# Feed of each state into PSUM, four normalisings on ScalarE, residues formed by TensorE, weights in two groups, and a new slot table, in a one-core hybrid of a state-space block, a gated recurrence and two expert layers

## Chip, core and metric

The program runs on one core of a Trainium2 chip. Time is device microseconds of one execution. All arrays are fp32, except a bf16 split of one small tile and the bf16 masks of the expert layers. TensorE is written PE, VectorE DVE, ScalarE ACT, GpSimd POOL and SyncE SP.

## What is computed

The input x is 16 batches of 512 tokens of 128 features. Each batch passes four stages; only the core of each is shown.

```python
# A: state-space block
xn = x * rsqrt(mean(x*x) + 1e-5) * norm_w      # of x already layer-normalised
u, res = split(xn @ in_proj_w.T, 2)
u_c = silu(causal_conv4(u))                    # 256 channels
dt_r, Bm, Cm = split(u_c @ x_proj_w.T)         # 8, 16, 16
delta = softplus(dt_r @ dt_w.T + dt_b)
for n in 16 states:                            # scan along the 512 tokens
    h[n] = exp(delta * A[n]) * h[n] + (delta * u_c) * Bm[n]
y = sum_n(h[n] * Cm[n]) + u_c * Dp
out = (y * silu(res)) @ out_proj_w.T + x
z = gelu(out @ ff_w1.T) @ ff_w2.T + out;  a = layernorm(z) * w + b
# E (twice, called e1 and e2): one expert of 8192 for each of 8 heads, by product keys
q = layernorm(x) @ w_q;  pick = argmax over 32 keys, for 16 groups
x += sum_h( relu(score_h) * gelu(<w_down[pick_h], layernorm(x)>) * w_up[pick_h] )
# B: gated linear recurrence with 16 states, tanh, projection, layernorm (between e1 and e2)
```

## The kernel before

Every engine runs its own program over the same list of iterations (`run_pipeline`). Iteration i does phase PRE of batch i+1, phase CORE of batch i and phase POST of batch i-1 and of the three before it. An iteration has 64 slots (`TURN`), four for each state n of the scan. The table `SLOTS` gives each stage of each engine its slot, written out in the file; a slot of 64 or more means that the stage runs one or more iterations later. Thus five batches are in flight. `LAST_SLOTS` holds other slots for the last iterations, 16 to 19, in which only POST is left. An engine executes its own stages in slot order, one after the other, and waits on semaphores of the others. Slots of two engines are not tied together otherwise.

In PRE the batch is loaded and its statistics are taken. DVE normalises it (`dve_norm_x`, L1094), PE transposes it (L658) and forms the convolution as four matmuls for each half (L754), ACT applies silu, and PE projects to `dbl`. ACT writes `dbl` in bf16 into `split`, and POOL (`pool_rest`, L1335 and L1337) forms the two residues that make the bf16 split exact to three parts. POOL also forms `delta` (L1340) and `du` = delta * u_c (L1344).

In CORE, state n takes five steps. ACT forms dA = exp(delta * A[n]) (L925), four states ahead. PE spreads row n of B over all partitions into one of three PSUM banks `bcast` (`spread`, L716), and row n of C likewise; the three banks serve B and C in turn. In slot 4n DVE scans hp in place with dA (L1187), in slot 4n+1 it feeds the next state, hp = du * B (`feed`, L1177), and in slot 4n+2 it multiplies by C (L1196). For states 1, 9 and 11 POOL does that multiplication (L1318), from a copy of the row that ACT makes. PE adds the product to `ysum` through an identity matmul (L733). Four hp buffers rotate.

In POST the layernorms before e1, e2 and B are also applied by DVE (L1094). DVE finds the maxima (L1111, L1118) and the indices (L1126 to L1143). POOL issues 8 indirect DMAs for each of four token tiles and each expert layer, 64 in an iteration (L1305). DVE forms the dot products with the fetched rows (L1150), ACT scales the other half of each row (L907), and PE sums them (L692). Banks 0, 1 and 2 of PSUM are taken in turn by these stages; `claim` makes PE wait until the last user of a bank has been read.

All 37 weight loads come first. Setup waits for all of them, folds some weights (L534 to L564, PE L583 to L592), and only then does iteration -1 begin.

The few lines of the scan and the feed:

```python
nc.vector.tensor_tensor_scan(flat, dA[...], flat, 0.0, ALU.mult, ALU.add).then_inc(scanned, 1)
...
dve.wait_ge(b_spread, at(c, NS, n))
dve.wait_ge(y_sum, at(c, NS, before[-1]))
nc.vector.tensor_tensor(hp[:, BUFFER[n], :, :], src[:], spread_tile(0, n), ALU.mult).then_inc(fed, 1)
```

## Time and profile before

| what | value |
|---|---|
| median of three runs | 2453.9 us (2447.63 to 2456.02) |
| the profiled execution | 2438.47 us |
| its span, first to last instruction | 2436.5 us |
| mean granted TensorE clock | 0.859 of full speed |
| DVE busy | 2043.8 us, 84% |
| PE busy | 1641.8 us, 67% |
| POOL busy | 1572.4 us, 65% |
| ACT busy | 1322.6 us, 54% |

The profiled execution is 15 us shorter than the median of the three; 2 us of it lie outside the span. The shares are means over a start of some 70 us, a long middle, and an end of 354 us in which only POST is left. Busy time of an engine is a union: instructions of one engine overlap a little, so count times mean duration is more than it.

### The profile page before, as it was taken

What the parts mean: (1) busy time and instruction counts of PE and PEld (TensorE: products, weight loads), DVE (VectorE), ACT (ScalarE), POOL (GpSimd) and SP (SyncE); (2) the same over time, 40 slices, a digit from 0 to 9 for tenths busy, and PEclk for the clock granted to TensorE, in tenths of its full rate; (3) what the DMA queues carried; (4) which work ended last, traced back from release to release, by engine and by line L of the source; (5) the groups of instructions that cost most, each with busy time, mean ns of one, the idle gap of its engine ahead of it and who ended that gap; (6) DMA issues with size and microseconds to landing.
All of it is one profiled execution on the core that took longest, in us unless ns stands there. A gap on an engine that the chain in (4) does not pass through costs nothing.

```text
span 2436.5 us, 22230 instructions
## 1 busy us (share of the span) xinstructions
PE 1641.8 (67%) x5130; PEld 895.1 (37%) x5130; DVE 2043.8 (84%) x4871; ACT 1322.6 (54%) x2634; POOL 1572.4 (65%) x1175
## 2 busy tenths in 40 slices
PE   4677667677677867687787677787777767434532
PEld 2232334343334434343344344343444433322321
DVE  2899888899999999999999899999999898433332
ACT  2543555547475657575574757574766655212522
POOL 0135454686868686887868686868778786735344
PEclk9799898889898989998898889898999888766766
DMA  2001111121222222222212122222222121312122
GB/s 48 9 5 35 48 35 43 35 80 52 83 59 78 59 81 69 67 78 59 81 51 81 55 82 58 78 67 76 76 58 76 51 84 58 102 52 74 44 67 76
DMA packets 79859, 150.38 MB, mean 62 GB/s; under 512 B 20585, under 2 KB 46593, under 8 KB 79681
## 3 DMA queue, kind: packets, MB, share of 16 engines
q0 software_dynamic: 49152, 134.28, 19.1%
q1 hardware_dynamic: 28048, 13.90, 2.1%
q10 hardware_dynamic: 2544, 1.09, 0.3%
q14 instruction: 94, 0.76, 0.1%
q8 instruction: 21, 0.34, 0.1%
HBM read 145.01 MB, written 4.19 MB: 61 GB/s over the span
## 4 chain that ended last, share of the span: by engine, by line
DVE 33%; POOL 27%; issue 18%; PE 11%; ACT 4%; another core or an unknown queue 3%; DMA 1%; DVEq 0%; POOLq 0%; ACTq 0%
POOL rows L1305 24%; DVE hp L1187 8%; DVE rows L1150 5%; DVE hp L1177 3%; PE ysum L733 3%; DVE hp L1196 3%; PE bank L692 2%; DVE top L1111 2%; POOL hp L1318 2%; DVE mask L1132 2%; ACT rows L907 2%; DVE mask L1126 1%; PE bank L754 1%; DVE rank L1134 1%
## 5 line engine op out<-in xcount | busy, mean ns | idle before, releaser
L1305 POOL DMA_INDIRECT rows<-in_experts,index x1024 | 1276.4, 1246 | 428.0 <-issue 305.7
L733 PE MATMUL ysum<-hp,ident 128*128 128x512 f32 x1024 | 552.7, 667 | 120.3 <-POOL hp L1318 61.5
L1187 DVE TENSOR_TENSOR_SCAN hp<-dA,hp 128x1024 f32<-128x1024 f32 x256 | 591.2, 2309 | 7.4 <-issue 6.5
L925 ACT ACTIVATE dA<-delta,decay 128x511 f32<-128x511 f32 x512 | 334.9, 711 | 146.0 <-DVE hp L1187 101.2
L716 PE MATMUL bcast<-split,pick 128*128 128x512 bf16 x512 | 182.4, 409 | 288.4 <-DVE hp L1177 263.9
L1177 DVE TENSOR_TENSOR hp<-du,bcast 128x1024 f32<-128x1024 f32 x256 | 308.2, 1204 | 69.1 <-POOL du L1344 47.8
L1150 DVE CUSTOM_DVE_ANT_0 rows<-rows,xn 128x128 f32<-128x128 f32 x1024 | 303.8, 361 | 57.5 <-DMA rows<-in_experts,index 53.5
L733 PEld LDWEIGHTS ysum<-hp,ident 128*128 128x128 f32 x1024 | 211.1, 210 | 313.2 <-issue 145.4
L907 ACT ACTIVATE rows<-rows,coef 128x128 f32<-128x128 f32 x1024 | 307.6, 388 | 1.8 <-DVE coef L1157 1.8
L863 ACT ACT_TABLE_LOAD x215 | 275.8, 1283 | 15.4 <-PEq L500 11.7
L692 PE MATMUL bank<-rows,ident 128*128 128x256 f32 x1024 | 245.3, 395 | 42.0 <-ACT rows L907 42.0
L1196 DVE TENSOR_TENSOR hp<-hp,bcast 128x1024 f32<-128x1024 f32 x208 | 252.2, 1213 | 0.1
L1335 POOL TENSOR_TENSOR soft<-dbl,split 128x512 f32<-128x512 f32 x16 | 31.5, 1968 | 326.5 <-ACT split L1011 326.5
L692 PEld LDWEIGHTS bank<-rows,ident 128*128 128x128 f32 x1024 | 205.5, 201 | 73.9 <-ACT rows L907 42.5
L716 PEld LDWEIGHTS bcast<-split,pick 128*128 128x128 bf16 x512 | 52.0, 102 | 434.8 <-DVE hp L1177 318.8
L675 PE MATMUL bank<-w_sim,xnT 128*128 128x512 f32 x256 | 160.2, 712 | 17.7 <-DVE mask L1118 11.5
L1318 POOL TENSOR_TENSOR hp<-hp,c_row 128x1024 f32<-128x1024 f32 x48 | 121.6, 2533 | 32.7 <-ACT c_row L942 26.4
L868 ACT ACTIVATE ln<-mv,eps 128x4 f32<-128x4 f32 x48 | 14.3, 297 | 229.4 <-DVE mv L1080 147.5
L1111 DVE TENSOR_REDUCE top<-bank 128x16 f32<-128x512 f32 x128 | 86.5, 676 | 46.3 <-PE bank L675 42.8
L754 PE MATMUL bank<-xrT,w_taps 128*128 128x512 f32 x256 | 116.8, 599 | 1.6 <-ACT ucs L999 0.8
L1118 DVE TENSOR_TENSOR mask<-bank,top 128x512 bf16<-128x512 f32 x128 | 88.6, 692 | 13.1
L900 ACT ACTIVATE x<-bank 128x256 f32<-128x256 f32 x64 | 24.2, 379 | 133.5 <-PE bank L692 97.5
(171 smaller groups left out, 2267.6 us busy)
## 6 DMA issues: line engine op xcount, KB each, us to landing
rows<-in_experts,index POOLq DMA_INDIRECT x1024
x_in<-in_x SPq DMA_DIRECT2D x16, 256.0 KB
x_res<-in_x SPq DMA_DIRECT2D x16, 256.0 KB
y<-x SPq DMA_DIRECT2D x16, 256.0 KB
rows<-in_wq_t ACTq DMA_DIRECT2D x1, 512.0 KB
rows<-in_taps SPq DMA_DIRECT2D x1, 512.0 KB
rows<-in_in_proj_t SPq DMA_DIRECT2D x1, 256.0 KB
rows<-in_key_t SPq DMA_DIRECT2D x1, 128.0 KB
```

Source lines behind the costliest of these rows:

```text
L692: mm = nc.tensor.matmul(total, ident[:], e.rows[:, tiles, h, P:2 * P], start=False, stop=(h == HEADS - 1), skip_group_check=True)
L716: nc.tensor.matmul(bcast[k % NBC][:, 0, :], pick[:, r:r + 1].to_broadcast([P, P]), part[:], start=True, stop=True).then_inc((b_spread, c_s ...
L733: mm = nc.tensor.matmul(ysum[:, j, :], ident[:], hp[:, BUFFER[k], j, :], start=(k == 0), stop=(k == NS - 1))
L863: act.preload_act_table_set(name)
L907: op = nc.scalar.activation(row, row, ACT.Copy, scale=e.coef[:, t, h:h + 1])
L925: op = nc.scalar.activation(dA[:, n % NDA, j, 1:T], delta[q][:, j, 1:T], ACT.Exp, scale=decay[:, j, n:n + 1])
L1150: op = nc.vector.tensor_tensor_reduce(row, row, e.xn[:, t, :], 1.0, 0.0, ALU.mult, ALU.add, e.dot[:, t, h:h + 1])
L1177: nc.vector.tensor_tensor(hp[:, BUFFER[n], :, :], src[:], spread_tile(0, n), ALU.mult).then_inc(fed, 1)
L1187: nc.vector.tensor_tensor_scan(flat, dA[:, n % NDA, :, :].rearrange("p a b -> p (a b)"), flat, 0.0, ALU.mult, ALU.add).then_inc(scanned, 1)
L1196: nc.vector.tensor_tensor(state, state, spread_tile(1, n), ALU.mult).then_inc(read_out, 1)
L1305: pool.indirect_dma_start(e.rows[:, t, h, :], None, A["experts"], bass.IndirectOffsetOnAxis(ap=e.index[:, t, h:h + 1], axis=0)).then_inc(e ...
L1318: pool.tensor_tensor(state, state, c_row[:, k % NCR, :].unsqueeze(1).to_broadcast([P, NH, T]), ALU.mult).then_inc(pool_read, 1)
```

## The change

It has six parts.

1. **Feed.** `feed` writes du * B into a new PSUM tile of two banks, `fed_ps`, and the scan reads it there and writes hp. So the wait for `y_sum` moves from the feed to the scan, and the feed of state n+1 waits for the scan of state n. B has one PSUM bank (`b_ps`) and C one (`c_ps`), in place of three for both. Only two banks are left for all other stages: those of bank 2 move to bank 1, and the sum of e2 moves to bank 0.
2. **Normalising.** The four tiles xr, xn of e1, xn of e2 and xnb are written by ACT (`Identity` with scale and bias). DVE only forms the bias, -mean * scale.
3. **Residues.** PE subtracts the bf16 parts in the PSUM bank of `dbl` with a matmul by minus the identity (`pe_rest`), and ACT reads them there. POOL's two subtractions go. The dt matmuls now follow the two residues in bank 0.
4. **Loads.** Eleven loads that PRE needs come first. The other 26 are issued by SP as iteration -1 begins. Folding is done by PE and DVE at the end of iteration -1, and the taps are scaled in its slot 6.
5. **Smaller setup.** Only the first column of dA is cleared.
6. **Slot tables.** All of `SLOTS` and `LAST_SLOTS` is new.

```diff
+        b_ps = ctx.enter_context(nc.psum_tensor("b_ps", [P, 1, T], F32))
+        c_ps = ctx.enter_context(nc.psum_tensor("c_ps", [P, 1, T], F32))
+        fed_ps = ctx.enter_context(nc.psum_tensor("fed_ps", [P, NH, T], F32))
-        bank = [ctx.enter_context(nc.psum_tensor(f"bank{k}", [P, T], F32)) for k in range(3)]
+        bank = [ctx.enter_context(nc.psum_tensor(f"bank{k}", [P, T], F32)) for k in range(2)]
...
     # DVE, feed
+                    if n:
+                        dve.wait_ge(scanned, at(c, NS, n - 1))
-                    nc.vector.tensor_tensor(hp[:, BUFFER[n], :, :], src[:], spread_tile(0, n),
+                    nc.vector.tensor_tensor(fed_ps[:], src[:], b_ps[:].to_broadcast([P, NH, T]),
                                             ALU.mult).then_inc(fed, 1)
     # DVE, scan
+                        if before:
+                            dve.wait_ge(y_sum, at(c, NS, before[-1]))
-                        nc.vector.tensor_tensor_scan(flat, dA[:, n % NDA, :, :].rearrange("p a b -> p (a b)"), flat,
-                                                     0.0, ALU.mult, ALU.add).then_inc(scanned, 1)
+                        nc.vector.tensor_tensor_scan(flat, dA[:, n % NDA, :, :].rearrange("p a b -> p (a b)"),
+                                                     fed_ps[:].rearrange("p a b -> p (a b)"), 0.0, ALU.mult,
+                                                     ALU.add).then_inc(scanned, 1)
...
     # PE, slot 4n
-                        for k in range(2 * n + 3, min(2 * n + 5, 2 * NS)):
-                            spread(c, split[q], k)
+                        spread_c(c, split[q], n)
+                        if n + 1 < NS:
+                            spread_b(c, split[q], n + 1)
...
+                    for m, r, k in due("pe_rest", i, q, slot):
+                        claim(0, i)
+                        nc.tensor.matmul(bank[0][:], minus[:], split[r][:], start=False, stop=True,
+                                         skip_group_check=True).then_inc(rest_mm, 1)
+                        fill(0, i, m, "pe_rest", k, (part2, split_done)[k], 1)
...
     # ACT
+                    for m, r, _ in due("act_norm_x", i, q, slot):
+                        act.wait_ge(p_shifted, at(m, 1))
+                        if later(m):
+                            act.wait_ge(p_turned, at(m - 1, 1))
+                        normalise(xr, x_in, s20, offx, p_normed)
...
     # slots that the text speaks of
-    "pe_sum_e2": (POST, (243, 250)),
+    "pe_sum_e2": (POST, (248, 248)),
-    "dve_dot_e1": (POST, (61, 71, 76, 80)),
+    "dve_dot_e1": (POST, (56, 74, 76, 77)),
-    "dve_index_e2": (POST, (194, 203)),
+    "dve_index_e2": (POST, (177, 191)),
-    "pool_rest": (PRE, (35,)),
-    "pool_delta": (PRE, (48,)),
+    "pool_delta": (PRE, (50,)),
-    "pool_x1": (POST, (0,)),
-    "pool_x3": (POST, (113,)),
-    "pool_fetch_e1": (POST, (37, 47, 51, 52)),
+    "pool_x1": (POST, (11,)),
+    "pool_x3": (POST, (124,)),
+    "pool_fetch_e1": (POST, (42, 44, 52, 53)),
```

## Rows read from the trace of the kernel before

**Rows 1.** The page, part 2: DVE's busy tenths in 40 slices of the span.
```profile
DVE  2899888899999999999999899999999898433332
```

**Rows 2.** Stretches: us, then busy us (instructions) of PE, PEld, DVE, ACT, POOL.
```profile
0.00:73.50 73.50, 31.02 (x78) 16.51 (x78) 16.57 (x57) 24.33 (x37) 8.26 (x11) 0.85 0.20 40
...
758.80:1824.90 1066.10, 800.18 (x2546) 439.98 (x2545) 1025.60 (x2417) 665.59 (x1320) 807.46 (x585) 0.90 0.24 69
...
2082.60:2436.50 353.90, 132.62 (x440) 89.14 (x438) 118.45 (x613) 102.94 (x271) 169.11 (x176) 0.67 0.24 68
```

**Rows 3.** DVE's groups, 758.8 to 1824.9 us: busy us, mean ns, idle before.
```profile
L1187 DVE TENSOR_TENSOR_SCAN hp<-dA,hp 128x1024 f32<-128x1024 f32 x128 | 292.3, 2283 | 6.5 <-issue 6.5
L1150 DVE CUSTOM_DVE_ANT_0 rows<-rows,xn 128x128 f32<-128x128 f32 x512 | 162.2, 382 | 14.0 <-DMA rows<-in_experts,index 14.0
L1177 DVE TENSOR_TENSOR hp<-du,bcast 128x1024 f32<-128x1024 f32 x128 | 154.3, 1206 | 3.3 <-PE bcast L716 3.0
...
L1132 DVE TENSOR_TENSOR mask<-mask 128x512 bf16<-128x512 bf16 x32 | 25.5, 797 | 1.1
...
L1094 DVE TENSOR_SCALAR xr<-x_in,mv,s 128x128 f32<-128x128 f32 x32 | 20.4, 714 | 0.3
L1094 DVE TENSOR_SCALAR xn<-x,mv,rs 128x128 f32<-128x128 f32 x64 | 18.6, 372 | 0.0
...
L1094 DVE TENSOR_SCALAR xnb<-x,mvB,rsB 128x128 f32<-128x128 f32 x32 | 8.8, 370 | 0.0
```

**Rows 4.** DVE's groups over the whole span: the small bias instruction.
```profile
L1088 DVE SCALAR_TENSOR_TENSOR off<-mv,rs 128x4 f32<-128x4 f32 x16 | 2.5, 157 | 0.0
```

**Rows 5.** Single lines over the whole span: ns min/median/max, first and last start.
```profile
L1150 DVE CUSTOM_DVE_ANT_0 rows<-rows,xn x1024: 258/286/4226, 241.4 to 2417.1; 128x128 f32<-128x128 f32 x171
...
L1132 DVE TENSOR_TENSOR mask<-mask x64: 424/426/2641, 210.2 to 2382.6; 128x512 bf16<-128x512 bf16 x64
...
L1305 POOL DMA_INDIRECT rows<-in_experts,index x1024: 943/949/3087, 214.9 to 2411.9; - x171
```

**Rows 6.** Timeline of DVE and POOL: start us, duration us, engine, line.
```profile
781.12 2.28 DVE L1187 TENSOR_TENSOR_SCAN hp<-dA,hp 128x1024 f32<-128x1024 f32 x1
783.32 0.66 DVE L1111 TENSOR_REDUCE top<-bank 128x16 f32<-128x512 f32 x1
784.09 0.69 DVE L1118 TENSOR_TENSOR mask<-bank,top 128x512 bf16<-128x512 f32 x1
...
781.71 2.44 POOL L1305 DMA_INDIRECT rows<-in_experts,index  x1 [0.31 <-issue]
...
882.97 2.42 POOL L1344 TENSOR_TENSOR du<-delta,ucs 128x1024 f32<-128x1024 f32 x1 [0.16 <-POOL delta L1340]
...
883.12 2.42 DVE L1150 CUSTOM_DVE_ANT_0 rows<-rows,xn 128x128 f32<-128x128 f32 x1
```

**Rows 7.** POOL's groups, 758.8 to 1824.9 us.
```profile
L1305 POOL DMA_INDIRECT rows<-in_experts,index x513 | 665.4, 1297 | 167.7 <-issue 148.2 <-DVE index L1143 18.9
...
L1335 POOL TENSOR_TENSOR soft<-dbl,split 128x512 f32<-128x512 f32 x8 | 14.0, 1750 | 83.5 <-ACT split L1011 83.5
```

**Rows 8.** ACT's and PE's groups, 758.8 to 1824.9 us.
```profile
L875 ACT ACTIVATE xn<-x_in,off,rs 128x128 f32<-128x128 f32 x32 | 13.1, 478 | 0.0
...
L733 PE MATMUL ysum<-hp,ident 128*128 128x512 f32 x513 | 275.9, 665 | 46.8 <-DVE hp L1196 29.6 <-POOL hp L1318 17.0
...
L716 PE MATMUL bcast<-split,pick 128*128 128x512 bf16 x256 | 89.5, 401 | 141.4 <-DVE hp L1177 132.8 <-issue 8.3
```

**Rows 9.** Timeline of the start: start us, duration us, engine, line.
```profile
15.97 0.49 DVE L534 TENSOR_SCALAR rows<-rows,norm_w 128x512 f32<-128x512 f32 x1 [7.14 <-DMA w_xproj<-in_xproj_t]
...
28.18 0.87 DVE L1075 BATCH_NORM_STATS2 st<-x_in 128x6 f32<-128x128 f32 x4 [0.32 <-PEq L500]
...
34.30 5.16 PE L754 MATMUL bank<-xrT,w_taps 128*128 128x512 f32 x8 [0.78 <-ACT xrT L993]
...
73.54 2.29 DVE L1187 TENSOR_TENSOR_SCAN hp<-dA,hp 128x1024 f32<-128x1024 f32 x1 [0.53 <-ACT dA L925]
```

625 lines of the change are left out of this document (324 added, 301 removed).

## The prediction, made before the changed kernel was seen to run

> **What bounds the kernel now.** I read the page's slices first: DVE is busy nine tenths or more in nearly every slice from the seventh to the 33rd, and drops to three or four tenths at the end [rows 1]. So there are three stretches, and I asked for the busy time of each [rows 2]. In the middle I took 758.8 to 1824.9 us. It holds 128 scans, 16 to an iteration, so eight iterations of 1066.1 / 8 = 133.3 us [rows 2, 3]. DVE is busy 1025.6 / 8 = 128.2 us of each and idle 5.1. PE is busy 100 us, POOL 101, ACT 83. DVE sets the pace of the middle. At the start (73.5 us) all engines together follow one chain from the weights to the first scan. At the end (354 us) no engine is busy half the time: that is a chain of latencies, and DVE's work is only 118 us of it [rows 2].
>
> Second, POOL is fuller than it looks. Between two indirect DMAs of the same group lie 0.3 us of issue that count as idle: 64 x (1.297 + 0.30) = 102 us, with 101 - 64 x 1.297 = 18 us of other work 120, and a wait of 83.5 / 8 = 10.4 us at the first residue [rows 7]. Together that is the iteration.
>
> Third, DVE and POOL stop each other. An indirect DMA takes 949 ns in the median but 1297 on average, and up to 3087 [rows 5, 7]; the one that starts 0.6 us into a scan takes 2.44 us and ends after it [rows 6]. In the other direction, a dot product takes 286 ns in the median, 382 on average; the one that starts beside POOL's `du` takes 2.42 us [rows 5, 6]. In both cases the DVE instruction has two inputs in SBUF. Feed and C product, one input in PSUM, take 1206 ns without such cases [rows 3].
>
> **The change, part by part.** Per iteration of the middle, on DVE:
>
> Normalising. The three groups are busy 20.4 + 18.6 + 8.8 = 47.8 us in eight iterations, 6.0 each [rows 3]. Each of the four sets overlaps the next instruction by some 0.1 us, as the scan does (next start 2.20 after its own, duration 2.28 [rows 6]), so 5.5 us go. This contains the stops of xr (714 ns against 372 of xn). Four small instructions come, 4 x 0.157 = 0.6 us [rows 4], less overlap: +0.5. ACT gets 16 instructions of 478 ns at most [rows 8], 7.6 us beside its 50 idle ones, so they cost nothing there. On the chain to the transposes they are 0.4 to 0.8 us slower a set; those chains have a state of slack or more in the middle. With that cover gone, at the end, three sets for each of four batches cost up to 10 us.
>
> Stops of DVE by POOL. The dots lose 512 x (382 - 286) = 49.2 us in the eight iterations, the mask maximum 32 x (797 - 426) = 11.9 [rows 3, 5]: 7.6 us an iteration. They happen where POOL's tensor products meet dots or masks. Two of POOL's eight products go (residues). The new table puts the first dots at slot 56 behind `pool_delta` at 50, where they were at 61 behind 48, and the others at 10, 12, 13 away from the products of slots 0 and 4, which now fall into scans. But `pool_x1` at 11 is beside the dots, and `dve_index_e2` at 49 and 63 is beside `pool_delta` and `pool_x3`. I can't see the new meeting points, so: bounds 0 and 7.6, and I take 5, since the scan no longer shifts POOL's work to random places.
>
> Scan and feed. If one input in SBUF does not stop POOL, as feed and C product show, the 348 ns of mean excess go from each DMA: 64 x 0.348 = 22 us of POOL, and with the residues (about 3 us and the wait of 10) POOL falls from 133 to about 97 us. That shortens nothing by itself; it makes fetches early. The Trainium skill, page "SBUF — State Buffer", section "Who interferes with whom", states that a DVE instruction with two SBUF inputs contends with a GpSimd instruction that reads SBUF and one with a single SBUF input outside the two-port modes does not; the trace agrees, with the 2.44 us above.
>
> The price of a PSUM output or of a scan out of PSUM is in no row. The nearest are feed and C product, 1206 to 1213 ns with PSUM in, for 1024 elements, where the scan of two SBUF inputs has 2283; nothing in them asks for more than 15 ns. I take +15 ns on 32 instructions, 0.5 us; bounds 0 and 0.1 us each, 3.2 us. The feed must wait for the scan before it. Where it stands right behind it, it loses the overlap of 0.08 and gains a gap of 0.11, as the mask behind the maximum does (783.32 + 0.66 to 784.09 [rows 6]): 0.19. By the new table twelve of sixteen slots 4n have another DVE stage between them: 4 x 0.19 = 0.8 us. The upper bound is 16 x 0.19 = 3.0.
>
> PE. Spreads were a whole state ahead; DVE waited for them only 3.0 us in eight iterations [rows 3], while PE waited 132.8 us for feeds [rows 8]. Now B of n+1 can be spread only in slot 4n, behind the C product of n-1, and is wanted right after scan n. PE has 2.28 us for two spreads of 0.4, so 1.4 to spare, and the other stages of slot 4n; what it still has to do of earlier slots must fit in. A state has 8.3 us, PE's mean work is 6.3, of which `ysum` is some 2. States 4 (skip and a convolution half) and 14 (both halves of e2's sum, 18 matmuls, then y) are heavier than their DVE time by 2 to 3 us. I put +3 us on DVE's idle time of 5.1; bounds 0 and 12. The residue matmuls add two of the spread's kind, under 1 us, to PE.
>
> Sum per iteration: -5.5 + 0.5 - 5 + 0.5 + 0.8 + 3 = **-5.7 us**, so 127.6 us. Eleven iterations of that kind: -63. The filling ones before have fewer POST stages; five at half of it or a little more: -14. The last one with a scan: -5. Middle: -82.
>
> Start. Statistics begin at 28.18, held by the loads (15.97) and the folding [rows 9]. After, setup ends when six DMAs per queue and 4 us of memsets are done: about 6. From there to the first convolution matmul it took 34.30 - 28.18 = 6.1. Now the taps stand in between: 11 loads, the last issued at about 4 instead of 11 us, land some 5 us later, at 9; tap scaling 2 us; shift, ACT set, transpose and copy 4 more: convolution at about 15.3, which is -19. The residues move in front of dt: two rounds of a spread-like matmul and an ACT copy of 0.6, +2.3. Folding took 28.2 - 16.0 = 12 us; it now lies behind PE's dt matmuls and beside ACT's exp and log and POOL's two products, which hide all but some 2 us (all 12 if that cover is gone). Start: -15. The 26 later loads are issued by SP while nothing waits for it.
>
> End. Other slots, sums of three stages in one bank, a slower ACT set, but nothing whose size I can read: 0, bounds -15 and +15.
>
> Total: -82 - 15 = **-97 us**. Against the profiled execution that is 2438.5 - 97 = 2341; against the median, 15 us higher, **2357 us**.
>
> **Rivals.** *More of the same* (0.15): all stops go (-2.6 more) and idle stays at 5.1 (-3): 5.6 x 17 = 95 us more at most, half of it likelier: 2262 to 2310. *The stops only move* (0.12): POOL's products meet other dots; the 5 us stay, +85: 2437. The table speaks for it, since `pool_x1`, `pool_x3` and `pool_delta` still have two-input neighbours. Here also stands the case that the scan goes on stopping POOL. *PSUM has a price* (0.08): the 0.1 us of the bound, 2.7 us more an iteration, +45: 2402. The Trainium skill, page "VectorE: DVE Perf Modes", section on the TRN2 errata, gives 62 more fixed cycles to an instruction from PSUM than to one from SBUF; by that estimate 65 ns on 32 instructions give 2.1 us an iteration. Our rows of PSUM inputs do not bear it out, and no row has a PSUM output.
>
> *PE is late* (0.10), the case on the other side. With one bank for B and one for C, every wait of PE for ACT (sigmoid, tanh, residues, bank 1 held by five stages in turn) that comes before slot 4n delays feed and C product. Without idle growth the gain is 97 + 3 x 17 = 148 us, or 148 / 256 = 0.58 us for each state. If DVE waits longer than that on average, 9 us an iteration, the kernel is slower. Four late states of 3 us would do: 12 us, then 2454 - 148 + 12 x 17 = 2510. PE's 33 idle us speak against it, the lost lead of a state for it.
>
> **Numbers.** The forecast's own case, 2315 to 2400, has 0.52; the rivals 0.45; 0.03 is left for no change. The measurement of this kernel can't tell less than about 0.3%, 7 us, from nothing. Only the late PE ends above; the moved stops end at -0.7%. Faster 0.87, same 0.03, slower 0.10. The range of 8 in 10 goes from half of "more" to the moved stops: 2290 to 2435.
>
> **What would show it.** In the changed profile: iterations near 127 us; no L1305-like DMA above 1.3 us beside a scan, mean near 0.97; POOL's issue-corrected time near 97 us; mean dot near 310 ns; scan and feed within 30 ns of 2283 and 1206; DVE waiting for spreads some 3 us an iteration; first scan near 58 us; the end near 354. Wrong would make me: DVE idle above 14 us an iteration with PE as releaser, scans above 2.4 us, or dots as slow as before.

## The result: 12.9% slower here, and what the profile after shows

The changed kernel took 2764.51 us (median of four runs, 2761.82 to 2767.47) against 2450.77 for the kernel before beside it: 1.129 times as long, 95% interval 1.124 to 1.134. The forecast was 2357 us, with 0.87 on faster. It was wrong, and by far. The jobs of this study (a job is one set of kernels run side by side on one chip) fell under two conditions: under the first, called starving below, the kernel before took 2444 to 2454 us and the changed kernel 1.129 of it; under the second, called free, they took 2366 us and 0.941 of it, and all runs of a kernel in a job lay within 1%.

The first lines are of the page of the changed kernel, part 2 (busy tenths in 40 slices, cf. [rows 1]) and part 4 (who ends the chain).

```profile
DVE  3898999594986759578585957759597785834331
...
issue 4%; DVE 3%; PE 3%; ACT 2%; another core or an unknown queue 1%; POOL 1%; DMA 0%; ACTq 0%; POOLq 0%; DVEq 0%
```

VectorE was full from the seventh slice on; now it falls to five tenths every few slices. The chain adds up to 15% of the span only (97% in the kernel before), so nothing more is read from it. The next view has stretches of the same kernel, in the columns of [rows 2]: eight iterations, then one uninterrupted run of 32 indirect DMAs inside one of them, then the 6 us behind that run.

```profile
794.80:2099.00 1304.20, 826.79 (x2520) 446.37 (x2560) 968.07 (x2322) 693.16 (x1433) 607.57 (x568) 0.84 0.20 57
1140.20:1180.00 39.80, 12.38 (x55) 7.23 (x54) 16.54 (x68) 9.76 (x21) 30.35 (x32) 0.75 0.36 102
1180.00:1186.00 6.00, 0.00 (x0) 0.00 (x0) 0.51 (x3) 1.34 (x2) 0.04 (x1) 0.50 0.08 25
```

An iteration is 1304.2 / 8 = 163.0 us instead of 133.3. VectorE works 968.1 / 8 = 121.0 of it, 7.2 us less than before (forecast 8.7); but it is idle for 42.0. POOL works 76. In the 39.8 us in which POOL issues 32 DMAs, VectorE is busy 16.5, TensorE 12.4 and ScalarE 9.8: each is idle for more than half of it, and the granted clock falls with them to the lower level behind it (0.50).

The groups of VectorE and POOL in the eight iterations, in the columns of [rows 3] and [rows 7]:

```profile
L1235 DVE TENSOR_TENSOR_SCAN hp<-dA,fed_ps 128x1024 f32<-128x1024 f32 x128 | 291.5, 2278 | 5.0 <-issue 3.2 <-ACT dA L920 1.8
L1219 DVE TENSOR_TENSOR fed_ps<-du,b_ps 128x1024 f32<-128x1024 f32 x129 | 157.9, 1224 | 48.7 <-remote 37.5 <-PE b_ps L686 7.9
L1245 DVE TENSOR_TENSOR hp<-hp,c_ps 128x1024 f32<-128x1024 f32 x104 | 125.9, 1210 | 57.0 <-remote 44.3 <-issue 12.7
L1156 DVE CUSTOM_DVE_ANT_0 rows<-rows,xn 128x128 f32<-128x128 f32 x512 | 117.6, 287 | 61.4 <-issue 61.3
...
L1156 DVE DVE_READ_ACCUMULATOR2_ANT dot<- 128x1 f32 x512 | 42.1, 82 | 54.5 <-issue 54.5
```

```profile
L1350 POOL DMA_INDIRECT rows<-in_experts,index x512 | 493.4, 964 | 207.8 <-issue 148.0 <-DVE index L1149 57.9 <-DVE hp L1235 0.6
```

The durations are those of the forecast: scan 2278 (before 2283), dot 287 (382), indirect DMA 964 (1297). The idle time is what is new, and its releasers are not engines: "issue" and "remote" mean that the profile shows nothing of this core that the instruction waited for. They are weaker evidence than they look: in this trace most records of semaphore events are missing (see "What stays open"). TensorE as releaser has 7.9 us in eight iterations. The timeline of VectorE in that run of 32 (start us, duration us) shows what it looks like:

```profile
1153.36 0.29 DVE L1156 CUSTOM_DVE_ANT_0 rows<-rows,xn 128x128 f32<-128x128 f32 x1
1153.57 0.08 DVE L1156 DVE_READ_ACCUMULATOR2_ANT dot<- 128x1 f32 x1
1153.75 0.29 DVE L1156 CUSTOM_DVE_ANT_0 rows<-rows,xn 128x128 f32<-128x128 f32 x1
1155.20 0.08 DVE L1156 DVE_READ_ACCUMULATOR2_ANT dot<- 128x1 f32 x1 [1.16 <-issue]
...
1173.43 0.08 DVE L1156 DVE_READ_ACCUMULATOR2_ANT dot<- 128x1 f32 x1 [1.12 <-issue]
1174.82 0.29 DVE L1156 CUSTOM_DVE_ANT_0 rows<-rows,xn 128x128 f32<-128x128 f32 x1 [1.31 <-issue]
1176.24 0.08 DVE L1156 DVE_READ_ACCUMULATOR2_ANT dot<- 128x1 f32 x1 [1.12 <-issue]
1185.49 0.89 DVE L1088 BATCH_NORM_STATS2 stC<-bank 128x6 f32<-128x128 f32 x4 [9.17 <-remote]
```

Until 1153.6, 13.4 us into POOL's run, dots follow each other every 0.21 us. Then one instruction starts every 1.40 us (1173.43, 1174.82, 1176.24), although the rows have landed. The run ends at 1180.0; at 1185.5 the engine works normally again. The same happens at each run of 32, VectorE idle for 23.1 to 23.6 us in it and 5.4 to 5.6 after; a run of 16 costs 7.6 to 8.1 + 3.1, or 4.5 + 2.1 where one of its DMAs was stopped, one of 8 some 0.5. Together that is 38 us an iteration.

**Theory A:** a long uninterrupted run of indirect DMAs starves the other engines. In the kernel before, scans with two inputs in SBUF stopped POOL every 8 us and so cut its runs to 8 or fewer; the feed into PSUM took that brake away. ("Cut" means here that a DMA is stopped, not that POOL pauses: by the traces both kernels issue 32, 16, 8 and 8 DMAs in an iteration with 0.3 us between them. In the kernel before 6 or 7 of the 32 are stopped and take some 1.9 to 3.1 us, no more than 8 follow one another unstopped, and the row takes 49 to 51 us; in the changed kernel none is stopped and it takes 39.8.) **Theory B:** the single-bank spreads, TensorE's order or the merged banks cause the idle time, which falls beside the runs by chance.

### The profile page after: what moved, and what is told of

Read it like the earlier page. It is cut to its first block and busy times, and to the rows that moved or that the text cites. A ratio compares the mean times of both kernels' runs of the same rounds, so it can differ in the third digit from the quotient of the medians.

```text
span 2760.0 us, 22210 instructions
## 1 busy us (share of the span) xinstructions
PE 1688.4 (61%) x5088; PEld 907.6 (33%) x5162; DVE 1947.9 (71%) x4680; ACT 1382.0 (50%) x2859; POOL 1215.6 (44%) x1143
## 5 line engine op out<-in xcount | busy, mean ns | idle before, releaser
L1350 POOL DMA_INDIRECT rows<-in_experts,index x1024 | 986.1, 963 | 487.7 <-issue 300.2
L1235 DVE TENSOR_TENSOR_SCAN hp<-dA,fed_ps 128x1024 f32<-128x1024 f32 x256 | 583.1, 2278 | 5.5 <-issue 3.2
L1219 DVE TENSOR_TENSOR fed_ps<-du,b_ps 128x1024 f32<-128x1024 f32 x256 | 313.4, 1224 | 90.6 <-remote 52.8
L1156 DVE CUSTOM_DVE_ANT_0 rows<-rows,xn 128x128 f32<-128x128 f32 x1024 | 241.0, 294 | 132.9 <-issue 105.7
L1245 DVE TENSOR_TENSOR hp<-hp,c_ps 128x1024 f32<-128x1024 f32 x208 | 251.9, 1211 | 80.6 <-remote 57.2
L626 PE MATMUL bank<-w_y_ln,xnbT 128*128 128x128 f32 x128 | 42.8, 438 | 389.5 <-DVE stC L1088 378.1
L626 PEld LDWEIGHTS bank<-w_y_ln,xnbT 128*128 128x128 f32 x128 | 34.0, 326 | 400.5 <-DVE stC L1088 388.9
L686 PE MATMUL b_ps<-split,pick 128*128 128x512 bf16 x255 | 108.9, 427 | 71.2 <-DVE fed_ps L1219 48.9
L1156 DVE DVE_READ_ACCUMULATOR2_ANT dot<- 128x1 f32 x1024 | 84.2, 82 | 89.2 <-issue 89.2
L733 PE MATMUL bank<-xrT,w_taps 128*128 128x512 f32 x256 | 128.4, 648 | 23.1 <-issue 12.0
L695 PE MATMUL c_ps<-split,pick 128*128 128x512 bf16 x184 | 79.5, 432 | 81.7 <-DVE hp L1245 80.6
## 6 DMA issues: line engine op xcount, KB each, us to landing
rows<-in_key_t SPq DMA_DIRECT2D x1, 128.0 KB, 5.0
```

The costliest lines, as they stand in the source:

```text
L733: mm = nc.tensor.matmul(bank[0][:], w_taps[:, tap, k * P:(k + 1) * P], xrT[:, tap:tap + T], start=(tap == 0), stop=(tap == NK - 1))
L1156: op = nc.vector.tensor_tensor_reduce(row, row, e.xn[:, t, :], 1.0, 0.0, ALU.mult, ALU.add, e.dot[:, t, h:h + 1])
L1219: nc.vector.tensor_tensor(fed_ps[:], src[:], b_ps[:].to_broadcast([P, NH, T]), ALU.mult).then_inc(fed, 1)
L1235: nc.vector.tensor_tensor_scan(flat, dA[:, n % NDA, :, :].rearrange("p a b -> p (a b)"), fed_ps[:].rearrange("p a b -> p (a b)"), 0.0, ALU ...
L1245: nc.vector.tensor_tensor(state, state, c_ps[:].to_broadcast([P, NH, T]), ALU.mult).then_inc(read_out, 1)
L1350: pool.indirect_dma_start(e.rows[:, t, h, :], None, A["experts"], bass.IndirectOffsetOnAxis(ap=e.index[:, t, h:h + 1], axis=0)).then_inc(e ...
```

## Experiments

Each job compared its kernels with the kernel before on the same chip. The last column is the stretch of us behind the last gate, from the profile; a gate is the product with silu(res), once a batch (L1290 in the kernel before, L1335 in the changed one). Job 0 is the comparison above.

| job | kernel before | run | ratio (95% interval) | per iteration | end |
|---|---|---|---|---|---|
| 0 | 2450.8 | the changed kernel | 1.129 (1.124-1.134) | 163.0 | 340 |
| 1 | 2366.0 | e1_sbuf_feed | 0.968 (0.966-0.970) | 127.5 | 274 |
| 1 | | e2_paced | 1.262 (1.260-1.264) | 169 | 434 |
| 1 | | e3_before_paced | 1.348 (1.346-1.351) | 183 | 442 |
| 1 | | e4_tied | 1.012 (1.010-1.014) | 138.2 | 272 |
| 2 | 2444.0 | e5_pause4 | 0.989 (0.988-0.991) | 132.6 | 337 |
| 2 | | e6_pair_each | 1.773 (1.770-1.776) | 253 | 680 |
| 2 | | e7_pause1 | 0.951 (0.948-0.954) | 126.5 | 319 |
| 3 | 2452.1 | e8_pause1_core | 0.960 (0.957-0.964) | 126.5 | 333 |
| 3 | | e9_drain_core | 0.956 (0.953-0.959) | 128.0 | 337 |
| 3 | | e10_before_core | 1.086 (1.083-1.090) | 149.2 | 350 |
| 4 | 2365.7 | e11_after_again | 0.941 (0.939-0.942) | 124.9 | 270 |
| 4 | | e12_sbuf_again | 0.970 (0.968-0.973) | 128.2 | 276 |
| 4 | | e13_pause16 | 0.950 (0.948-0.951) | 124.5 | 293 |
| 4 | | e14_before_end | 1.021 (1.020-1.023) | 133.1 | 332 |
| 5 | 2365.5 | e15_pause16_again | 0.951 (0.949-0.952) | 124.7 | 294 |

m1_bench ran in job 2, m2_bench in job 3, m3_bench_again in job 5, each once. Jobs 0, 2 and 3 fell under the starving condition, jobs 1, 4 and 5 under the free one.

### Job 1: feed back in SBUF, pauses, fetches tied to scans

e1_sbuf_feed undoes one part of the change:

```diff
-nc.vector.tensor_tensor(fed_ps[:], src[:], b_ps[:].to_broadcast([P, NH, T]),
+dve.wait_ge(y_sum, ...)          # as in the kernel before
+nc.vector.tensor_tensor(hp[:, BUFFER[n], :, :], src[:], b_ps[:].to_broadcast([P, NH, T]),
                         ALU.mult).then_inc(fed, 1)
```

> The changed kernel with one part undone: the feed writes its product in place into the state's tile in SBUF, so that the scan reads both its inputs from SBUF again (and the feed waits for the state's output again); the PSUM spreads, the normalising on ScalarE, the residues and the slot table stay those of the changed kernel. Theory A: VectorE's idle time of 40 us in an iteration comes from GpSimd, which nothing stops any more, so that it issues 16 or 32 indirect DMAs in one uninterrupted run; from about 12 us into such a run all other engines nearly cease to be given instructions. Scans with two SBUF inputs stop GpSimd again for some 2.3 us each, every 7.7 us, so the runs are cut into pieces of at most 8 DMAs: iterations of 130 to 137 us instead of 159 to 167, time 2380 to 2460 us. Theory B: the idle time comes from the single-bank spreads, the order of TensorE's work or the merged banks: all of these are still there, so the iterations stay at 155 us or more and the time at 2680 to 2780 us.

e2_paced adds pauses to the changed kernel, e3_before_paced the same to the kernel before:

```diff
                 for h in range(HEADS):
                     pool.indirect_dma_start(...)
+                for _ in range(20):
+                    pool.memset(pause[:], 0.0)
+                    pool.drain()
```

> The changed kernel with one addition: after each 8 indirect DMAs GpSimd clears a small tile of its own 20 times, with a drain after each, a pause estimated at 3 to 8 us (8 pauses in an iteration, 24 to 64 us of GpSimd, which is idle over 80 us of each iteration). Nothing else is changed; the outputs are the same. Theory A (uninterrupted runs of indirect DMAs starve all engines from about 12 us on): no run lasts longer than 10 us before its pause, so VectorE's idle time of 40 us in an iteration goes to 8 to 15 us, iterations are 128 to 138 us, and the time 2330 to 2450 us, faster than the changed kernel by 300 us or more although only work was added. Theory B (spreads, TensorE's order, banks): a pause on GpSimd can only make rows later: 2760 us or more. If the pause is too short to let the other engines recover, something between, with the idle time per run smaller than 28 us for the run of 32.

> The kernel before with the same addition: after each 8 indirect DMAs GpSimd clears a small tile 20 times with a drain after each. Theory A: in its iterations the scans already cut the runs into pieces of 8, so the pauses give nothing there (GpSimd is busy 101 us of 132, and 8 pauses of 3 to 8 us can make its rows late: 0 to +100 us in all); but at its end, where no scan runs, a run of 32 DMAs left VectorE idle for 32 us, and with pauses this run costs 10 to 20 us less. So the end from the last gate on, 354 us, gets shorter by 10 to 25 us. Theory B: the end stays at 354 us or gets longer by the pauses.

e4_tied:

```diff
                     for m, r, t in due("pool_fetch_e2", i, q, slot):
+                        if CORE in has:
+                            pool.wait_ge(scanned, at(b[CORE], NS, n))
                         fetch(e2, m, t)
```

> The changed kernel with one addition: in the iterations each group of 8 indirect DMAs first waits for the scan of its slot's state, and the four groups of the second expert layer are set at slots 204, 212, 220 and 222 instead of 206, 211, 221 and 222, so that the groups come at least one state (7.5 us) apart where the table puts them apart; no pause lies between groups whose slots are of one state. Theory A: runs of 32 go away, leaving runs of at most 16 (7.6 us idle within and 3 after for one of 16): VectorE idle 12 to 25 us in an iteration instead of 40, time 2380 to 2560 us. Theory B: groups that start later can only make the dots later: 2760 us or more.

The SBUF feed gave 0.968, on the side of theory A but better than it had: iterations of 127.5 us (130 to 137 expected), 2289 us (2380 to 2460). The pauses came out slower than anything theory A allowed. POOL's timeline explains that: the first drain behind DMAs takes some 2.1 us, each further pair 0.30, so 20 pairs cost 8 us; eight of them an iteration, 64 us, on top of POOL's own 95 make 159 of 169 us. Both paced kernels were bound by POOL; the end of e3_before_paced, 442 us, tells nothing of starving for the same reason. At this point I read the job as for theory A, in particular because "issue" and "remote" as VectorE's releasers had vanished in e2_paced. That reading was too early, as job 4 shows: job 1 was under the free condition, where the changed kernel has only 3 us of such idle time an iteration without pauses either. For the same reason neither e1_sbuf_feed nor e4_tied tells the theories apart here. What e4_tied does show is a price: groups tied to scans make rows late (VectorE waits 96 us in eight iterations for fetched rows), 138.2 us an iteration.

### Job 2: shorter pauses, and a small kernel of dense streams

The same edit with 4 pairs after each 8 DMAs, with 1 pair after each 8, and with 1 pair after every DMA.

> The changed kernel with a pause of 4 clear-and-drain pairs after each 8 indirect DMAs (20 pairs took 8.5 us, so 4 take an estimated 1.7 us; 8 pauses in an iteration add 14 us to GpSimd's 76). Theory A: if 1.7 us is enough for the other engines to be supplied again, VectorE's waits named issue and remote (some 38 us in an iteration) vanish and rows are late by little: iterations of 125 to 135 us, ratio to the kernel before 0.95 to 1.00. Theory A': the supply needs the 5 us that passed after the end of each run before the engines went on: then 1.7 us brings back only a part, ratio 1.03 to 1.12. Theory B (20 pairs took the idle away by another way, such as GpSimd being late): a ratio of 1.10 or more.

> The changed kernel with a single clear-and-drain pair (0.43 us) after each 8 indirect DMAs. If any gap between DMAs resets the starving: starved time near zero, ratio 0.95 to 0.99, the best of the paced ones. If the gap must be as long as a stalled supply needs: starved time of 25 to 38 us an iteration, ratio 1.07 to 1.13.

> The changed kernel with one clear-and-drain pair (0.43 us) after every indirect DMA, so that a DMA starts each 1.7 us instead of each 1.25 and a run of 32 lasts 54 us instead of 40; 64 pairs add 27 us to GpSimd's 76 of an iteration. Theory A with the mean rate as the cause (each DMA uses up some of a budget that refills with time): the starved time falls but the rows are later: ratio 0.97 to 1.08. Theory A with the bare back-to-back issue as the cause (any other instruction on GpSimd between two DMAs lets the others in): starved time zero, ratio 0.95 to 1.00. If neither rate nor gaps matter: 1.12 or more.

A single pair after each 8 DMAs, which only adds work, has a ratio of 0.951 (2319 us) where the changed kernel without it had 1.129. The stretch of eight iterations in it, and what one pause is on POOL:

```profile
731.40:1743.00 1011.60, 781.02 (x2560) 409.25 (x2560) 940.48 (x2322) 694.32 (x1433) 619.62 (x632) 0.96 0.25 73
```

```profile
1324.21 0.95 POOL L1351 DMA_INDIRECT rows<-in_experts,index  x1 [0.30 <-issue]
1325.16 0.20 POOL L1355 MEMSET pause<- 128x100 f32 x1
1327.52 2.35 POOL L1369 TENSOR_TENSOR hp<-hp,c_row 128x1024 f32<-128x1024 f32 x1 [2.17 <-issue]
```

The iteration is 126.5 us, VectorE idle for (1011.6 - 940.5) / 8 = 8.9 of it. A gap of 2.6 us between groups of 8 DMAs takes away 33 us of idle time. Four pairs, 3.5 us, already make rows late (132.6 us); a pair after every DMA makes each DMA 3.5 us long, 64 x 3.5 = 224 us of POOL, and the iteration 253: 1.773, far above the 0.95 to 1.08 that I expected, so this run says nothing of starving.

The small kernel m1_bench has nothing of the reference in it; its output is only zeros. In stages it starts three streams of independent short instructions together with a run of 32 indirect DMAs:

```diff
+for j in range(ops):    # VectorE, 0.13 us each; ScalarE and TensorE alike
+    nc.vector.tensor_reduce(out_dve[:, j:j + 1], src[:, 0:width], AX_X, ALU.add)
```

> A small kernel of its own (the output is only zeros; nothing of the reference is computed): stages, each started together on all engines, in which GpSimd issues 32 indirect DMAs (128 rows of 1 KB each) while VectorE, ScalarE and TensorE work through streams of short instructions that wait for nothing. A row of an expert table is read as before. Stages: no DMA; 32 DMAs beside all three dense streams; 32 beside 40 wide reductions (1024 elements, some 1.1 us each) on VectorE alone; 32 beside 400 narrow ones on VectorE alone; 32 with rows of 128 B; 32 with 2 or 5 clear-and-drain pairs after each 8; 32 with one pair after each. Theory A1 (a long run holds up the supply of instructions, and each engine lives on what it has fetched): the narrow streams stop some 5 to 15 us into the run and go on after it (a stage of 30 us becomes 45 to 60 us), the 40 wide reductions take the same 44 us as without DMAs or at most 3 us more; pauses restore the supply. Theory A2 (the run stops any instruction, however long): wide reductions show gaps too, 10 us or more in all. Theory A3 (the bytes do it): rows of 128 B leave the streams undisturbed, against A1 and A2, by which the number of DMAs counts and the narrow rows disturb as much. Theory B (nothing of this is from the DMAs): all stages of dense streams take the same time within 2 us.

Windows of it: no DMA; 32 DMAs beside the three streams (the run alone, then the whole stage); 32 beside 40 wide reductions alone; beside 400 narrow ones alone; rows of 128 B; 2 pairs and 5 pairs after each 8 DMAs; one pair after each DMA.

```profile
3.20:50.90 47.70, 47.69 (x400) 47.53 (x400) 38.08 (x300) 22.00 (x150) 0.00 (x0) 1.00 0.01 2
51.00:91.10 40.10, 13.00 (x73) 11.18 (x74) 13.21 (x84) 14.97 (x80) 30.41 (x32) 0.62 0.35 102
51.00:135.00 84.00, 52.53 (x400) 50.39 (x400) 40.94 (x300) 25.73 (x150) 30.41 (x32) 0.76 0.17 51
148.80:194.00 45.20, 0.49 (x2) 0.30 (x2) 45.16 (x40) 0.26 (x1) 30.26 (x32) 0.54 0.32 93
194.00:272.60 78.60, 0.80 (x2) 0.50 (x2) 54.02 (x401) 0.27 (x2) 30.26 (x32) 0.50 0.19 54
289.20:372.30 83.10, 56.36 (x400) 52.53 (x400) 42.09 (x300) 26.24 (x150) 30.20 (x32) 0.75 0.05 7
386.10:451.60 65.50, 53.73 (x400) 51.57 (x400) 40.38 (x300) 23.54 (x150) 31.78 (x40) 0.90 0.23 65
465.40:533.40 68.00, 53.99 (x400) 51.89 (x400) 40.48 (x300) 23.54 (x150) 33.98 (x52) 0.90 0.22 63
547.20:661.50 114.30, 44.93 (x400) 44.74 (x400) 38.09 (x300) 22.01 (x150) 36.70 (x64) 0.71 0.13 38
```

In the 40 us of the run VectorE starts 84 of its 300 instructions, which it works off in 38 us without DMAs. These streams wait for no semaphore and for no bank, so theory B can't be what stops them. The 40 wide reductions run on without a gap (45.16 busy of 45.20); but the narrow ones on VectorE alone had their first gap only after 88, so 40 may have been too few to see one. Rows of 128 B starve as much as rows of 1 KB (83.1 us against 84.0, at 7 GB/s against 51): bytes are not it; both have the same number of DMAs and of fetched rows. With a pair after each DMA all streams are at full speed. Pauses after each 8 give back only about half (65.5 and 68.0 us, against 84.0 without and 47.7 without DMAs), less than I expected and less than in the real kernel. VectorE, some lines at the end of the run of 32, which ends at 91.1:

```profile
86.40 0.22 DVE L87 TENSOR_REDUCE out_dve<-src 128x1 f32<-128x64 f32 x1 [1.18 <-issue]
87.80 0.22 DVE L87 TENSOR_REDUCE out_dve<-src 128x1 f32<-128x64 f32 x1 [1.18 <-issue]
...
94.80 0.22 DVE L87 TENSOR_REDUCE out_dve<-src 128x1 f32<-128x64 f32 x1 [1.18 <-issue]
96.20 4.90 DVE L87 TENSOR_REDUCE out_dve<-src 128x1 f32<-128x64 f32 x38 [1.18 <-issue]
```

One instruction each 1.40 us, and 5 us behind the run the dense stream is back: the period and the tail of the changed kernel.

### Job 3: where the pauses belong, and the length of a run

e8_pause1_core pauses only `if CORE in has`; e9_drain_core has the drain without the clearing; e10_before_core is the kernel before with the pair of e8.

> The changed kernel with one clear-and-drain pair after each 8 indirect DMAs in the iterations only; behind the last iteration, where 16 groups of 8 DMAs follow one another and GpSimd sets the pace, there is no pause. With a pair everywhere the stretch behind the last gate took 318.9 us; without pauses, with the PSUM feed, 271.8 us. Theory A: the iterations stay as with a pair everywhere (126 to 129 us) and the end goes to 270 to 280 us: ratio 0.93 to 0.94. If starving costs the end as much as the pauses do (theory A with a costly end): 0.945 to 0.955.

> The same with only the drain, no clearing: GpSimd waits some 2.1 us for the DMAs that it has sent and goes on. If the wait for landing is what lets the others in: as with the pair, ratio 0.925 to 0.94, iterations 125 to 128 us. If another instruction of the engine between the DMAs is what does it: starved time comes back, ratio 1.05 to 1.13.

> The kernel before with one clear-and-drain pair after each 8 indirect DMAs in the iterations only. Its GpSimd is busy 101 us of 133 in an iteration, and 8 pauses of 2.6 us make 122 with its gaps some 130. Theory A (starving costs the kernel before nothing in its iterations, since the scans cut the runs): ratio 1.00 to 1.05, by GpSimd being later. Theory C (the kernel before loses by starving too, and a pause alone gives what was gained, whatever the change): ratio 0.95 to 0.98.

The drain alone does as well as the pair (0.956 and 0.960), so the wait for landing is what matters. Leaving the end unpaced did not pay: 333 us against 319, so starving costs the end more than the pauses do, and my 270 to 280 was wrong. All three ratios lie above what was expected. The kernel before gets 8.6% slower by pauses, where theory A had at most 5% (and theory C, by which a pause alone would help it, 2 to 5% faster): its POOL has no room (8 x 2.3 us on top of the forecast's 120, and scans still stretch its DMAs), so the cure needs the POOL time that the change sets free.

> The small kernel of its own again (output only zeros) with other stages: runs of 8, 12, 16 and 64 indirect DMAs beside dense streams on VectorE, ScalarE and TensorE; 32 beside VectorE and ScalarE alone; 32 beside 80 reductions of 512 elements (0.6 us each) on VectorE alone; 32 with a wait for landing after each 8 (no drain, no other instruction); 32 with a clearing of 256 elements after each, without drains; and 32 clearings of 512 elements without any DMA. Theory A1 (a budget of instructions that a run eats up): no gap or a few in the run of 8, gaps from 6 to 7 us into each longer run, with no end in the run of 64; two streams start to starve later (8 to 11 us) than three; reductions of 0.6 us are held up only where one is given each 1.4 us or 0.7 us; clearings alone hold up nothing; waiting for the landing cures most. If a slower rate alone cures: the run with clearings between shows no gap. If only an empty queue cures: it shows gaps from 8 to 12 us on.

Windows of m2_bench: runs of 8, 12, 16 and 64 beside three streams, the middle 40 us of the run of 64, a wait for landing after each 8, a clearing after each DMA (one DMA each 1.5 us), 32 clearings of POOL without a DMA.

```profile
63.70:115.00 51.30, 47.25 (x400) 46.62 (x400) 38.89 (x300) 22.62 (x150) 7.74 (x8) 0.97 0.08 22
128.80:186.20 57.40, 48.42 (x400) 47.65 (x400) 39.40 (x300) 23.63 (x150) 11.37 (x12) 0.91 0.10 29
200.00:263.60 63.60, 49.67 (x400) 48.80 (x400) 39.81 (x300) 24.09 (x150) 15.14 (x16) 0.87 0.12 34
277.40:404.80 127.40, 55.78 (x400) 52.82 (x400) 56.89 (x400) 29.17 (x150) 60.63 (x64) 0.67 0.23 67
317.50:357.50 40.00, 5.28 (x15) 4.03 (x14) 6.37 (x29) 7.43 (x29) 30.32 (x32) 0.50 0.37 105
...
560.60:626.70 66.10, 53.56 (x400) 51.37 (x400) 41.20 (x300) 23.77 (x150) 30.31 (x32) 0.90 0.23 65
640.50:719.60 79.10, 59.82 (x400) 53.72 (x400) 42.15 (x300) 27.33 (x150) 40.99 (x64) 0.76 0.19 54
733.40:778.30 44.90, 44.85 (x400) 44.74 (x400) 38.09 (x300) 22.02 (x150) 15.02 (x32) 1.00 0.01 2
```

A run of 8 costs the three streams some 6 us (51.3 against 44.9), one of 16 costs 19, one of 64 costs TensorE's stream 82: there is no end to it. In the steady part each engine starts 29 instructions in 40 us, one per 1.4. A slower rate without a gap helps a little (79.1 against 84.0), waits after each 8 help more (66.1), but again by half only. The 80 reductions of 0.6 us on VectorE alone showed no gap, and with 80 of them the stage may again have been too short. POOL being busy is not it: clearings disturb nobody.

### Jobs 4 and 5: the same kernels under the other condition

That job 1 had a faster kernel before, and ends of 274 and 272 us in two variants against 340 in job 0, asked for the plainest experiment: the changed kernel, unedited, beside the one with the SBUF feed.

> The changed kernel, nothing edited, beside the kernel with the feed in SBUF on one chip. Theory A with the chip of no account: ratio 1.12 to 1.14 and some 40 us of VectorE's idle time in an iteration again. If another chip starves less: a ratio nearer to 1, with the same runs of 32 DMAs but less idle time in each.

> The kernel with the feed back in SBUF once more. If its 0.9676 holds on this chip, 0.96 to 0.975 and iterations of 127 us; the difference to the changed kernel beside it is then the cost of the free GpSimd. If the first chip made it look good: 0.98 to 1.02.

The changed kernel took 2225.7 us, **0.941** of the kernel before. Eight iterations, one uninterrupted run of 32 in them, and the end:

```profile
711.20:1710.50 999.30, 784.43 (x2520) 422.25 (x2560) 951.89 (x2322) 693.54 (x1433) 607.37 (x569) 0.94 0.26 74
850.70:890.70 40.00, 31.54 (x113) 17.60 (x114) 38.54 (x130) 32.09 (x78) 30.51 (x32) 0.96 0.35 102
1953.40:2223.60 270.20, 118.64 (x430) 78.90 (x430) 105.88 (x578) 106.17 (x290) 157.09 (x163) 0.75 0.29 82
```

The 32 DMAs are issued just as fast (40.0 us, 102 GB/s), and VectorE is busy 38.5 of the 40 instead of 16.5. So under this condition a run starves nobody. VectorE is idle for (999.3 - 951.9) / 8 = 5.9 us an iteration, with the single-bank spreads, the merged banks and the slot table all in place: what theory B blamed costs nothing of the 42 us. The small kernel says the same:

> The first small kernel again, nothing edited (the output is only zeros). On a chip on which the kernel before takes 2366 us: if such a chip does not starve its engines, all stages of dense streams take the time of the stage without DMAs (VectorE 38 us, ScalarE 22 us) within 2 us, a run of 32 beside them or not; if it starves too but only denser streams show it, the numbers of the first time come back (72 us and 55 us). On a chip on which it takes 2444 us or more: 72 us and 55 us again.

```profile
50.10:95.10 45.00, 44.93 (x400) 44.74 (x400) 38.09 (x300) 22.01 (x150) 30.41 (x32) 1.00 0.33 95
154.00:204.90 50.90, 0.86 (x3) 0.57 (x3) 50.84 (x401) 0.34 (x2) 30.26 (x32) 0.50 0.30 83
220.40:265.40 45.00, 44.94 (x401) 44.75 (x401) 38.10 (x301) 22.02 (x151) 30.19 (x32) 1.00 0.09 13
```

Beside 32 DMAs, alone or with narrow rows, no stream has a gap: 45.0 us where the same instructions took 84.0.

> The changed kernel with one clear-and-drain pair after each 16 indirect DMAs (each 8: 0.951; none: 1.129). An unbroken run of 16 left VectorE idle for 8.1 us within and 3.1 us after, and there are 4 in an iteration where all groups follow one another; by that 15 to 30 us an iteration stay: ratio 1.00 to 1.06. If the state that starves needs more than 16 DMAs to set in, and it was its pile-up over 32 that cost: ratio 0.945 to 0.96.

> The kernel before with one clear-and-drain pair after each 8 indirect DMAs only behind its last iteration, where nothing cuts the runs. Theory A: its end of 354 us gets 10 to 30 us shorter, although 16 pauses of 2.6 us are added to the engine that sets the pace there: ratio 0.988 to 0.996. If GpSimd alone sets the end and starving costs it nothing: 20 to 40 us longer, ratio 1.008 to 1.016.

> The changed kernel with one clear-and-drain pair after each 16 indirect DMAs, once more. On a chip of the 2366 us kind 0.950 again. On one of the other kind: each of the runs of 16 starves for some 8 to 11 us where the dense streams starved for 10 us in a run of 16, so 0.98 to 1.04; if most of what was lost in the run of 32 comes after the 16th DMA, 0.955 to 0.975.

Here pauses can only cost, and they do: a pause after each 16 brings 0.950 (0.951 again) instead of 0.941, 20.5 us, all of it in the end (293 against 270). Pauses in the end of the kernel before cost 50 us. So e14_before_end did not test its question, which needed the other condition; nor did e13 and e15, so what a run of 16 costs in the real kernel is known only from the changed kernel's own 7.6 to 8.1 + 3.1 us.

The end of the kernel before answers in another way. Its last gate is at 2082.6 us in the first profile and at 2083.0 in e14_before_end, whose iterations are unedited; but the whole takes 73 us less in job 4 than that profiled execution (85 less than the median beside it). With 2 us outside the span, its end is 2365.7 - 2.0 - 2083.0 = 280.7 us there against 353.9 [rows 2]: 73.2 us. And the chain of the kernel before, as first profiled, has these steps in its end (start us, us):

```profile
2092.01 21.47 another core or an unknown queue
...
2124.40 21.34 another core or an unknown queue
...
2208.59 7.83 another core or an unknown queue
2216.82 15.79 another core or an unknown queue
2234.32 7.38 another core or an unknown queue
```

They sum to 73.8 us; that this equals the 73.2 is in part luck, since some of each step would be there anyway. The first two lie in and around a run of 32 DMAs (2100.3 to 2140.1), the others in and behind two runs of 16 (2199.6 to 2240.5). So the kernel before was starved too, only where no scan stopped its DMAs: in its iterations, with the same 32 in a row but 6 or 7 of them stopped, VectorE is idle for 0.4 to 4.7 us in the row under the starving condition and under the free one (e14_before_end), and the iteration takes 133.3 and 133.1 us. That it is the stopping that protects is read from this comparison alone; the feed back in SBUF was never run under the starving condition. Under the free one e12 has 7 stopped DMAs of the 32, the changed kernel none.

## Why the prediction was wrong, step by step

**The step that failed** is "Scan and feed": POOL falls to about 97 us, and "that shortens nothing by itself; it makes fetches early". Both halves are true under the free condition. Under the starving one the first half is false: the stops that the step took away were the brake on POOL, and without them a row of 32 DMAs leaves VectorE idle for 23 + 5 us (0.4 to 4.7 with them). The rows themselves did not get longer; earliness is not what cost. With it failed the term "+3 us on DVE's idle time of 5.1", bounds 0 and 12: it measured +37 (42.0). None of the rivals was this one. "PE is late" ended on the right side, but its test, TensorE as releaser, has 1 us an iteration.

**The terms under the free condition** (e11_after_again; before: 133.1 an iteration) show which of the others were right:

- VectorE's work: 951.9 / 8 = 119.0 us, forecast 119.6. Dots 283 ns where I had 310; scan 2276 and feed 1222 for 2283 and 1206, so the price of PSUM is 16 ns on the feed and none on the scan, as taken. By the Trainium skill's page "VectorE: DVE Perf Modes", section on the TRN2 errata, it would have been an estimated 65 ns on the scan; no run shows that. The prediction put these 65 ns on 32 instructions; the page's figure is for an input from PSUM, and the feed had one already, so by the page only the 16 scans should have been counted.
- POOL: 64 x (0.963 + 0.30) + 14 = 95 us, forecast 97. e12 has the scan with two SBUF inputs and DMAs of 1245 ns beside it, e11 has 963. The stop was the feed's place, and the trace agrees with the rule of the Trainium skill's page "SBUF — State Buffer", section "Who interferes with whom", that the prediction weighed. The same section of the Trainium skill says that a DMA never contends with a compute engine. It speaks of SBUF's ports, and the starving is no case of that: the instructions keep their durations (dots 287 ns) and only start late.
- Idle: 5.9 us, forecast 8. Iteration: 124.9, forecast 127.6.
- Start: first scan at 58.96 us, forecast 58; before 73.54 [rows 9]. The first gate comes 12.0 us earlier (140.7 against 152.7), forecast 15.
- End: 270.2 against 280.7, forecast no change, bounds 15.
- Sum: -12.0 at the first gate, -117.6 in the iterations, -10.5 in the end, -140 us, forecast -97. That lies at the edge between the forecast's own case (down to 2315, -139) and the rival "more of the same" (2310 to 2262, -144 to -192), and its terms are that rival's: the stops all gone, the idle time near 5.1.
- A slip of the prediction: *the stops only move* is 2357 + 85 = 2442 us, not 2437; it bears on nothing here.

**The parts of the gain** by e12_sbuf_again: without the PSUM feed, 2295.6 us, so the feed is worth 70 us and all the rest of the change 70, under the free condition.

**What I could have seen.** The forecast put 0 for an end of 354 us that I called a chain of latencies, and left five steps of it, 73.8 us, to an "unknown queue". They stood in and behind runs of 16 and 32 DMAs of which none, or one, was stopped. The question "what happens in the middle if nothing stops POOL there either?" follows from these rows, and so does a rival with its price, an estimate: 21.47 + 21.34 = 42.8 us for one run of 32 in each of some twelve full iterations, 514 us, with which 2453.9 - 97 + 514 comes out at 2871, on the side where 2764 was measured. The price is too high: such a run cost VectorE 29 us.

**What stays open** is the mechanism and the condition. The starved engine gets one instruction each 1.40 or 0.70 us, whatever short instruction it is; it starts after 6.5 us with three dense streams, after 11 with one (49 and 88 of VectorE's instructions). Whether long instructions are held up alike is not shown, as said above.

*A dry supply of instructions.* The Trainium skill, page "Runtime: NRT & Kernel Launch", section "Instruction fetch mechanics", has instructions fetched in blocks of 16 KiB, 256 of them. The traces have such packets for TensorE's streams, and others of 8 KiB that come one for 128 of VectorE's instructions (16.1 us apart beside the dense stream of m3_bench_again). Under the starving condition they are as quick as under the free one: no instruction packet of m1_bench takes over 1.43 us, and in its stage with VectorE alone one lands at 203.2 us, 2 us before the first gap. So a slow fetch from memory is not it; what lies behind the fetch no trace shows.

*The recording.* Every time in this study comes with a span and a clock, so every execution was recorded, and under the starving condition the records themselves are incomplete. Of the landings of DMAs on semaphores (16 for each indirect DMA) the trace of the changed kernel holds 5232 in job 0 and 17722 in job 4; the kernel before has 11295 and its variant e14 17732. The part of the page with the DMA issues shows it too, since the time to landing stands there only if the landings do; job 0, then job 4:

```profile
rows<-in_experts,index POOLq DMA_INDIRECT x1024
...
rows<-in_experts,index POOLq DMA_INDIRECT x1024, 2.7
```

The records go missing in the same stretches in which the engines starve: in the middle 40 us of m2_bench's run of 64, 512 landings are due and 57 are there, one per 0.70 us, beside one instruction of VectorE per 1.40 us. All variants of jobs 2 and 3 lack landings, save e6_pair_each, in which DMAs are 3.5 us apart; none of jobs 1, 4 and 5 does. That the writing of records holds the engines up, and that the starving would be absent or smaller in an execution that nobody records, fits the DMAs counting and not their bytes, clearings doing no harm, and the tail behind a run. It is argued, not shown: a common cause of both would look the same, and the record has no run without recording. If it is so, the 12.9% are a loss that the measurement makes, and the 5.9% gain of job 4 tells more of the change.

Nor is it shown what sets the condition: each job was wholly in one of them, and two jobs whose chip bears the same number fell one on each side, so a lasting trait of a chip isn't shown.

## What to carry to other kernels

An engine that issues DMAs and is set free will issue them without a stop; ask what its brake was, and look in the chain for "unknown queue" or "issue" steps behind the densest rows it has already. Such steps, and DMA issues without a time to landing, can also mean that the trace lacks records: look at both before an idle stretch is explained. One wait for landing after each 8 indirect DMAs is an insurance if the engine has time to spare: here 0.951 instead of 1.129 where runs starve; where they don't, its price was not measured (after each 16 it is 0.950 against 0.941), and the kernel before, whose POOL was full, lost 8.6% by it. Before a cause is settled, run the unedited pair again in the job with the variants; one such run would have saved this study its first wrong reading.

## What the runs showed of the hardware that was not expected

- An uninterrupted run of GpSimd's indirect DMAs (one per 1.25 us, 128 rows each) can hold all other engines to one instruction per 1.40 us until 5 us behind its end, under a condition that three of the jobs had and that appears to come and go, in executions that are being recorded; the DMAs' own packets end as fast as ever, some 2.4 us after the start of each under both conditions.
- Bytes don't matter: 32 DMAs with rows of 128 B and of 1 KB starved alike (83.1 and 84.0 us).
- A trace taken under that condition lacks up to 70% of the DMA landings, and then names "issue", "remote" or an unknown queue as the releaser.
- The first drain on GpSimd behind indirect DMAs takes about 2.1 us, further ones 0.1 beside a clearing of 0.18; drained after every DMA, a fetch takes 3.5 us instead of 1.25.
